# The seventh image pair's rows scattered as pieces as well, and two gathers and sums begun some steps sooner

## The reference

```
h = tok(x)                                    # patch embedding, bias, positions
h = h + attn(layernorm(h))                    # 8 heads, softmax of K over tokens, of Q over channels
z = layernorm(h); logits = z @ gate_w + gate_b
top 2 of 16 experts per token, weights renormed to 1
out = h + sum over the two of  weight * ((silu(z @ w1[e]) * (z @ w2[e])) @ w3[e])
```

## Time and profile before

| | us |
|---|---|
| three runs | 754.32, 754.61, 757.6 |
| median | 754.61 |
| the profiled execution's own time | 757.5 |
| its span, first to last instruction | 755.7 |
| POOL busy | 503.5 (67%) |
| PE busy | 622.1 (82%) |
| DVE busy | 476.6 (63%) |
| ACT busy | 353.2 (47%) |

### The profile page before, as it was taken

One profiled execution on the slowest core, in us unless ns is written; L12 is line 12 of the kernel. 1 busy time (PEld: TensorE's weight loads), 2 busy tenths in 40 slices (PEclk: granted clock), 3 DMA queues, 4 the chain that ended last, 5 costly groups with the idle time before them and its releaser, 6 DMA issues.

```text
span 755.7 us, 13960 instructions
## 1 busy us (share of the span) xinstructions
PE 622.1 (82%) x4059; PEld 519.8 (69%) x4059; DVE 476.6 (63%) x1322; ACT 353.2 (47%) x774; POOL 503.5 (67%) x537
## 2 busy tenths in 40 slices
PE   5886687788979998999889998998894888799328
PEld 3365454666568967886779687967884787798228
DVE  5654645567556677767666756766585687598410
ACT  2121311226355647564656456545562557486400
POOL 4362044757577477777777777777777777777773
PEclk9958778589989999999999989998998789898755
DMA  3499504134184329542844284537351635664322
GB/s 82 90 175 345 203 29 111 49 108 120 56 226 132 95 55 230 136 131 65 208 134 131 62 204 120 135 82 165 92 149 57 164 98 158 175 150 98 68 59 59
DMA packets 169200, 94.52 MB, mean 125 GB/s; under 512 B 99551, under 2 KB 153207, under 8 KB 169129
## 3 DMA queue, kind: packets, MB, share of 16 engines
q1 hardware_dynamic: 152728, 67.65, 34.5%
q0 software_dynamic: 15616, 25.59, 12.8%
q10 hardware_dynamic: 784, 0.39, 0.2%
HBM read 45.40 MB, written 48.18 MB: 124 GB/s over the span
## 4 chain that ended last, share of the span: by engine, by line
PE 51%; DVE 20%; issue 9%; POOL 7%; DMA 6%; ACT 5%; ACTq 0%; SPq 0%; POOLq 0%; DVEq 0%
PE h_ps L1593 8%; PE wide_ps L1381 7%; PE y_ps L1614 5%; PE hidT_ps L1606 4%; PE turn_ps L1571 3%; PE wide_ps L1401 3%; DMA hx<-xi_scratch 2%; PE wide_ps L1504 2%; DVE twice_y L1298 2%; POOL rows_scratch L674 2%; POOL kexp L691 2%; POOL hx L691 2%; DMA xi_scratch<-xi 2%; PE wide_ps L1387 2%; ACT sums L860 2%
## 5 line engine op out<-in xcount | busy, mean ns | idle before, releaser
L674 POOL DMA_INDIRECT rows_scratch<-z_parts,place x224 | 224.5, 1002 | 126.9 <-issue 64.9
L691 POOL DMA_INDIRECT sums<-y_scratch,place x192 | 185.1, 964 | 66.2 <-issue 56.4
L1593 PE MATMUL h_ps<-w_hi,rowsT 128*128 (+1 forms) x388 | 117.8, 330 | 15.8 <-DVE hid_all L1300 15.4
L1298 DVE SCALAR_TENSOR_TENSOR twice_y<-tanh,h_ps 128x256 f32<-128x256 f32 (+1 forms) x194 | 80.4, 414 | 52.5 <-ACT tanh L818 31.2
L1593 PE MATMUL h_ps<-w_lo,rowsT 128*128 (+1 forms) x388 | 105.6, 298 | 0.0
L1614 PE MATMUL y_ps<-w_sb,hidT_all 128*128 (+1 forms) x776 | 103.1, 279 | 1.4 <-ACT twice_y L833 1.4
L1614 PEld LDWEIGHTS y_ps<-w_sb,hidT_all 128*128 128x128 f32 (+1 forms) x776 | 100.2, 202 | 2.3 <-issue 2.3
L1593 PEld LDWEIGHTS h_ps<-w_hi,rowsT 128*128 128x128 f32 (+1 forms) x388 | 78.8, 203 | 25.9 <-issue 22.3
L818 ACT ACTIVATE tanh<-h_ps 128x256 f32<-128x256 f32 (+1 forms) x194 | 69.6, 386 | 46.5 <-PE h_ps L1593 42.6
L1300 DVE SCALAR_TENSOR_TENSOR hid_all<-twice_y,h_ps 128x256 f32<-128x256 f32 (+1 forms) x194 | 81.6, 421 | 6.7
L1571 PE MATMUL turn_ps<-ident,rows_all 128*128 128x128 f32 (+1 forms) x388 | 64.4, 292 | 21.0 <-DMA rows_all<-rows_scratch 14.2
(11 more groups left out here) (350 smaller groups left out, 1107.0 us busy)
## 6 DMA issues: line engine op xcount, KB each, us to landing
rows_all<-rows_scratch SPq DMA_DIRECT2D x84, 256.0 KB
y_scratch<-twice_y SPq DMA_DIRECT2D x84, 128.0 KB
rows_scratch<-tanh SPq DMA_DIRECT2D x3, 3276.0 KB
xi_scratch<-xi SPq DMA_DIRECT2D x16, 256.0 KB
hx<-xi_scratch SPq DMA_DIRECT2D x14, 256.0 KB
rows_scratch<-z_parts,place POOLq DMA_INDIRECT x224
out<-sums SPq DMA_DIRECT2D x56, 64.0 KB
x_in<-in_x SPq DMA_DIRECT2D x26, 128.0 KB
```

Source lines behind the costliest of these rows:

```text
L674: gp.indirect_dma_start(rows_dram[n], bass.IndirectOffsetOnAxis(ap=place[m % RING][:, r, j:j + 1], axis=0), z_parts[m % 2][:, j // 2, j % ...
L691: gp.indirect_dma_start(y_of[r][apart(m)][:, j // 2, j % 2, :], None, y_dram[m % 3][0:GROUPS[m] * GROUP * width(m), :], bass.IndirectOffse ...
L1298: ve.scalar_tensor_tensor(twice[0:w, j, :], tanh[0:w, j, :], 1.0, halves[:, j, 0, :], ALU.add, ALU.mult).then_inc(S["twice_done"], 1)
L1593: mm = te.matmul(h_ps[0:w, j * 256:(j + 1) * 256], rowsT[g % 2][:, j * w:(j + 1) * w], w12[:, bass.ds(experts[g][j], 1), :, :].rearrange(" ...
```

## The change

The seventh pair (m = 6) joins PIECED. Its 32 row scatters become 16 piece scatters, one every half step from half step 169 (steps 85 to 92), where pair 7 keeps two every half step from 196. It gets 13 groups instead of 12, so START[7] is 85, there are 98 groups and the loop is a step longer. It is still gathered and summed in the old way, from tiles of 126 rows.

Pair 7's embedding and attention fill `wide_ps` in steps 79 to 91, so pair 6's piece columns are formed in `turn_ps` (even columns, right after `project_in`) and `hidT_ps` (odd columns, at the step's end). `turn` and `turn_hidden` now wait until ACT has copied the piece out, and `take_piece` stands ahead of `copy_hidT` on ACT. The start of each piece (`find_moves` on DVE) is taken out of `find_pieces` and, for pair 6, worked out half a step ahead of it, in `hidT_ps`; pair 6's sort ends two steps later than before (ends 19.5 for 17.5, owner 20 for 18), pair 7's mean is 1.5 steps later.

GATHER: pair 4's begins in step 86 instead of 91, pair 5's in 98 instead of 102, pair 6's stays at 111, pair 7's moves to 124. SUMS: pair 4's quarters are in steps 94 to 97 (99 to 102 before), pair 5's in 107 to 110 (112 to 115 before), pair 6's and 7's a step later. GATES is a step later.

```diff
-PIECED = (7,)
+PIECED = (6, 7)
...
-         LATER, LATER, LATER, LATER, LATER._replace(tiles=17.5, bases2=18, ends=18.5, owner=19))
+         LATER, LATER, LATER, LATER._replace(tiles=17.5, bases2=18.75, moves=19, ends=19.5, owner=20),
+         LATER._replace(mean=8, means=8.5, tiles=17.5, bases2=18, moves=18.5, ends=18.5, owner=19))
...
-ROUTES = (None, None, None, None, None, None, None, 196)
-
-GATES = 105
+ROUTES = {6: (169, 1), 7: (196, 2)}
+
+GATES = 106
...
-SCATTER = (16, 22, 28, 44, 59, 72, 85, None)
-GATHER = (38, 51, 65, 78, 91, 102, 111, 123)
-SUMS = ([[43 + 14 * m + q for q in range(4)] for m in range(5)]
-        + [[112, 113, 114, 115], [121, 122, 122, 123], [124, 125, 126, 127]])
+SCATTER = (16, 22, 28, 44, 59, 72, None, None)
+GATHER = (38, 51, 65, 78, 86, 98, 111, 124)
+SUMS = ([[43 + 14 * m + q for q in range(4)] for m in range(4)]
+        + [[94, 95, 96, 97], [107, 108, 109, 110], [122, 123, 123, 124], [125, 126, 127, 128]])
...
-        def piece_place(j):
-
-            return wide_ps[:, j % 2 * 512:(j % 2 + 1) * 512]
+        def in_between(m):
+
+            return m < PAIRS - 1
+
+        def piece_place(m, j):
+
+            return (turn_ps, hidT_ps)[j % 2][:, :] if in_between(m) else wide_ps[:, j % 2 * 512:(j % 2 + 1) * 512]
...
-                wait(pe, "route_ready", j + 1)
-                wait(pe, "piece_ready", j - 1)
+                if in_between(m):
+
+                    wait(pe, *(("rowsT_ready", g + 2), ("hidT_ready", g))[j % 2])
+                wait(pe, "route_ready", i + 1)
+                wait(pe, "piece_ready", i - 1)
...
                 wait(pe, "rowsT_ready", g)
+                wait_pieces(2 * (g - 2 + LAG) - 1)
...
                 wait(pe, "hidT_ready", g)
+                wait_pieces(2 * (g + LAG))
+                if g + LAG == step_of(PIECED[0], 18):
+                    wait(pe, "moves_ready", 2)
...
                 if 0 <= g < GROUPS_ALL:
                     activate(g)
+                for m, j in routes_at(2 * s - 1):
+                    take_piece(m, j)
                 if 0 <= g - 1 < GROUPS_ALL:
                     copy_hidT(g - 1)
```

More of the change, by code:

```diff
@@ L288, in vit_kernel @@
         moves = placed[0]
-        piece_at = sb("piece_at", [P, COLS], U32)
+        piece_at = [sb(f"piece_at{n}", [P, COLS], U32) for n in range(2)]
         piece_from = sb("piece_from", [P, COLS], U32)
@@ L309, in vit_kernel @@
         flat = (w_patch[:, :, :, :].rearrange("p j t e -> p (j t e)"), x_in0[:, :, :].rearrange("p r f -> p (r f)"),
-                x_cols0[:, :, :].rearrange("p j c -> p (j c)"), squares[:, :])
-        pieces = [place[:, n * one:(n + 1) * one] for place, count in zip(flat, (10, 2, 2, 2)) for n in range(count)]
-        assert len(pieces) == COLS and one == PIECE * P
+                x_cols0[:, :, :].rearrange("p j c -> p (j c)"))
+        pieces = [[place[:, n * one:(n + 1) * one] for place, count in zip(flat + (last,), (10, 2, 2, 2)) for n in range(count)]
+                  for last in (base0[:, :, :, :].rearrange("p t b e -> p (t b e)"), squares[:, :])]
+        assert len(pieces[0]) == COLS and one == PIECE * P
         x_in = (x_in0[:, :, :], twice_y[:, :].rearrange("p (r f) -> p r f", r=2))
@@ L359, in vit_kernel @@
         scattered = [sem(f"scattered{n}") for n in range(3)]
-        pieces_out = sem("pieces_out")
+        pieces_out = [sem(f"pieces_out{n}") for n in range(len(PIECED))]
         rows_in = [sem(f"rows_in{n}") for n in range(3)]
@@ L388, in routes_at @@
                 for j in range(COLS):
-                    if ROUTES[m] + j // 2 == half:
+                    if ROUTES[m][0] + j // ROUTES[m][1] == half:
                         yield m, j
@@ L835, in take_piece @@
             def take_piece(m, j):
-                wait(act, "piece_ps_ready", j + 1)
-                if j == 0:
+                wait(act, "piece_ps_ready", COLS * nth(m) + j + 1)
+                if j == 0 and nth(m) == 0:
                     wait(act, "emb_ps_ready", 2 * PAIRS)
+                    wait(act, "x_turned", PAIRS)
+                elif j == 0:
+                    wait_scattered(act, PIECED[0])
+                    wait(act, "logits_ps_ready", PAIRS)
+                if j == COLS - 4:
                     wait(act, "mean_ps_ready", PAIRS)
-                    wait(act, "x_turned", PAIRS)
-                    wait(act, "logits_ps_ready", PAIRS)
-                sc.activation(pieces[j][0:PIECES, :], piece_place(j)[0:PIECES, 0:PIECE * 2 * E], ACT.Copy).then_inc(S["piece_ready"], 1)
+                if j == COLS - 2:
+                    wait(act, "h2_ready", 3 * PAIRS)
+                sc.activation(pieces[nth(m)][j][0:PIECES, :], piece_place(m, j)[0:PIECES, 0:PIECE * 2 * E], ACT.Copy).then_inc(S["piece_ready"], 1)
             def take_gates(j):
@@ L847, in take_gates @@
                     wait_scattered(act, PAIRS - 1)
-                sc.activation(pieces[j][0:PIECES, :], piece_place(j)[0:PIECES, 0:PIECE * P], ACT.Copy).then_inc(S["gates_turned"], 1)
+                sc.activation(pieces[1][j][0:PIECES, :], piece_place(PAIRS - 1, j)[0:PIECES, 0:PIECE * P], ACT.Copy).then_inc(S["gates_turned"], 1)
             def weigh(m, q):
@@ L1200, in find_past, with find_moves @@
                 ve.tensor_scalar(past[:, :], tile_id[:, :], ends[:, 0:1], None, ALU.is_ge).then_inc(S["past_ready"], 1)
+            def find_moves(m):
+                i = nth(m)
+                wait(dve, "base_ps_ready", m + 1)
+                wait(dve, "place_summed", 2 * m)
+                wait(dve, "moved_ready", i)
+                lbs = piece_place(m, 1)[0:PIECES, :].rearrange("p (n j e) -> p n j e", n=2, e=EXPERTS)
+                ve.tensor_scalar(moves[0:PIECES], lbs[:, 0], piece_id[0:PIECES, 0:1], None, ALU.is_le).then_inc(S["moves_ready"], 1)
+                wait(dve, "moves_ready", 2 * i + 1)
+                ve.tensor_tensor(moves[0:PIECES], moves[0:PIECES], lbs[:, 1], ALU.mult).then_inc(S["moves_ready"], 1)
+                wait(dve, "moves_ready", 2 * i + 2)
+                wait(dve, "piece_at_ready", i)
+                ve.tensor_reduce(moved[0:PIECES, :], moves[0:PIECES], AX_X, ALU.add).then_inc(S["moved_ready"], 1)
             def find_places(m):
@@ L1230, in find_pieces @@
                 i, side_ps = nth(m), sides[second(m)]
+                wait(dve, "slot_u_ready", i)
                 wait(dve, "place_ready", m)
@@ L1624, in _ @@
                     project_in(g)
+                for m, j in routes_at(2 * s - 1):
+                    move_rows(m, j, g)
                 if 0 <= g - 1 < GROUPS_ALL:
```

83 lines of the change are left out of this document (43 added, 40 removed).

## The result

The changed kernel takes 778.2 us (771.04 to 786.32) where the kernel before, run beside it, takes 754.54: ratio 1.0272, 95% interval 1.017 to 1.0374. The ratio leaves out the run of 786.32, which lies more than 1.5% above the fastest; the other three have the median 774.03. It is slower; whether by 2% or more, the interval leaves open. The profiled execution is the one of 782.37 us, span 780.6, the longest of these three. In the traces of this document POOL's first pair-6 issue lies anywhere from 532.77 to 541.95 us, with the same tables ahead of it, so times counted from the start of the span differ by some 9 us from trace to trace, and lengths counted from that issue are the safer comparison.

The account below looks back on a forecast made before the run. POOL's full queue was taken to bound the kernel, with PE tied to it at two turns. Pair 7's turn at 678.7, then 17.6 + 4.9 + 40.3 + 30.18, gave span 771.7; less 2.9, plus 1.8: 771 us, range 757 to 782.

Parts of the forecast that it names:

- the rival of the worst banks: Steps 85 to 92 each grow by the full 2.6 us and pair 4's sums show fully: 781, chance 0.17.
- the two terms for the sums: Moved sums delay pair 7's first piece by 0 to 6.5 us (3.2 taken) and pair 6's gather by 4.9 (high 6.5).
- POOL is full, and its queue's order feeds PE: POOL's queue decides the end, PE waits for it at two turns; 22.1 us less POOL work turns into idle stretches.
- Pair 6's last piece: Steps 85 to 92: issued at 594.4 at the earliest, behind 15 pieces and 28 gathers, plus 2.6 us lateness (0 to 8).
- the third rival: Exchanging the two banks costs the worst: 781, chance 0.17; its sign is steps 85 to 92 taking over 62 us together.
- From the last piece to the turn: From pair 6's last piece to PE's turn of step 93: 5.66 us; turn at 602.7, bounds 599.4 and 608.
- From the turn to pair 7's first piece: From step 93's turn: 25.6 us as before plus 3.2 for pair 4's sums; piece at 631.5 (625.0 to 640.1).
- Pair 7's pieces among pair 5's gathers: 15 pieces and 18 gathers ahead of pair 7's last piece: 41.55 us, before 19.06; PE loses 31 us at the turn.
- The end: Pair 6's gather 17.6 plus 4.9 us after pair 7's turn, its 32 gathers 40.3, then 30.18: span 771.7.
- DVE against POOL: The 32 added DVE operations slow POOL's pair 6 pieces by 4 us at most; the skill's rule implied 8.
- A full POOL: Rival: POOL stays full, so the whole 22.1 us come off; span 733.6, time 732.5, chance 0.05.
- No change: Rival: the loss fits PE's slack, pair 7's first piece 18 us after step 93's turn; time 756, chance 0.08.

Follow-up runs that it names:

- the new order: Changed kernel with gathers of pairs 4 and 5 by columns, spread among and behind the pieces: 760.98 us; with the even piece later in its step, 749.91.
- the order back: Changed kernel with gathers and sums of the fifth and sixth pairs in the earlier kernel's steps: 771.83 us; with the even piece later too, 757.26.
- the best order found: Changed kernel with gathers of pairs 4 and 5 spread by columns and the even piece later in its step: 749.91 us, ratio 0.9948.

## Why the prediction was right, and where its size was off

The direction, the chain and the range (757 to 782) held. The forecast of 771 was 7 us short of the median of all four runs (778.2) and 3 us short of that of the three in the ratio (774.03), so the times don't tell it from the rival of the worst banks (781). The trace does, step by step; it is of an execution of 782.37 us, so its errors are the larger ones. That the time stayed in the range is in part luck: step 93's turn, at 615.0, lies 7 us past the prediction's upper bound of 608, and what saved the range is that the two terms for the sums, 6.5 us each at the high end, came out at 1.6 and 2.4. By the steps of the prediction:

- **POOL is full, and its queue's order feeds PE.** Right. POOL lost its 22.1 us of work. Of the idle stretches two were forecast with a size, 28 and 9 us, and came at 26.96 and 5.79; the third, at the pieces, was put into the lateness of 2.6 us and came at 12.5.
- **Pair 6's last piece: mis-sized, and this is the term that failed.** Forecast 594.4 + 2.6 = 597.0, with a lateness of 0 to 8; measured 609.26. POOL came to step 85 one us later than before and idled 12.5 us on pieces. The forecast took POOL's need for a pair of steps, 15 to 18 us, to say that PE is mostly ahead. That counts the gathers as cover; but ahead of the first gather in POOL's program stand four pieces with nothing between them, and there POOL needs 5 us for what took PE two steps (533.13 to 553.74). The growth of the eight steps was too small as well: 21 us was its worst case, 26.7 came. The worst case of 2.6 us a step is DVE's and ACT's added work. It leaves out PE's own added 1.0 us a step, though the same sentence works it out (the 48 matmuls of L1570 took 8.1 us), and PE's waits early in its step for ACT's copy of the rows, which the diff names (the wait on `rowsT_ready`), and for DVE's matrices, 12.8 us together, and PE's lower clock. The prediction's own sign for the third rival, over 62 us for these steps, was met with 69.8: as to the banks that rival was nearer than the forecast, and short as well. The experiments show which part is which: the place of the piece in its step is worth 13 of the 26.7 us. Of the whole time it is worth 11 us with the new order (760.98 to 749.91) and 15 with the order back (771.83 to 757.26); with the order as changed the difference (778.2 to 769.57) is not clear of the spread.
- **From the last piece to the turn**, 5.66 forecast, 5.74 measured: 2.55 for the scatter to land, 3.13 for the load.
- **From the turn to pair 7's first piece**, 28.8 forecast, 615.00 to 642.19 = 27.2 measured. If all of the 1.6 us over the 25.6 before are pair 4's sums, they show by that, not by 3.2, and not by the 6.5 that the third rival took.
- **Pair 7's pieces among pair 5's gathers**, 41.55 forecast, 683.88 - 642.19 = 41.69 measured; turn 5.63 later. The step with the most weight in the loss of PE's slack was exact.
- **The end.** Pair 6's gather at the turn + 20.0 (22.5 forecast), its 32 issues to 750.35 in 40.9 (40.3), the rest 30.25 (30.18). The errors add up: 12.3 - 1.6 + 0.1 - 2.5 + 0.6 + 0.1 = 9.0, which is 780.6 less 771.7, within rounding.
- **DVE against POOL.** Pair 6's pieces now run beside 32 added DVE operations. The piece scatters' durations (ns, min/median/max), before and now (ten pieces of pair 7; ten each of pairs 6 and 7):

```profile
L661 POOL DMA_INDIRECT rows_scratch<-w_patch,piece_at x10: 904/920/1166, 623.1 to 634.9; - x10
L667 POOL DMA_INDIRECT rows_scratch<-w_patch,piece_at x20: 907/930/1559, 541.3 to 664.0; - x20
```

The medians agree; one of the twenty took 1.56. The rule of the Trainium skill that was weighed there (SBUF — State Buffer, Who interferes with whom), that such a DVE operation and a GpSimd one shut each other out for the whole instruction, would have made it up to 8 us. The added operations of 0.52 us don't show it: away from longer DVE operations, POOL's issues beside them took 0.91 to 1.06. Operations of 1.22 us that are in both kernels do. From 300 us to pair 7's gather, 11 of POOL's issues in either trace took over 1.3 us, and each ran beside a TENSOR_TENSOR of 1024 columns with two SBUF inputs (11 of 13 such operations in either), as here on POOL and DVE of the changed kernel:

```profile
594.37 1.88 POOL L697 DMA_INDIRECT sums<-y_scratch,place  x1 [0.30 <-issue]
594.21 1.23 DVE L1111 TENSOR_TENSOR z_parts<-z,z_parts 128x1024 fp32r<-128x1024 f32 x1 [5.19 <-ACT z_parts L803]
```

POOL's issues beside a TENSOR_REDUCE of 1024 columns, which has one input, took 0.94 to 0.98. So the long operations with two inputs go with a DMA issue held back by 0.4 to 1.0 us; why the short ones don't, no run shows. The change adds none of the long ones, and the 4 us at most that the prediction allowed for DVE did not come.
- **The rivals.** A full POOL (732.5) needs its idle time to be nil; the best order found still leaves 17.3 us. No change (756) needs pair 7's first piece 18 us behind step 93's turn; it came 27 behind.

## What to carry to other kernels

An engine whose track looks 67% busy can be full: look at the gaps between its instructions before counting what an edit frees. Where such an engine issues in program order both what another engine waits for and what nobody needs yet, count what stands ahead of the awaited transfer, in units of one issue; that count gave the turns within 1 us where the order alone was changed, and missed by some 5 us in two of the kernels in which POOL waited for single pieces. A thin spread of the unurgent issues took the loss of 2.7% to 0.7%, and together with the later piece to a gain of 0.5%. Two delays that the same transfer waits for don't add up: undoing one shows little until the other is gone. Before a bank that is exchanged between two uses is put first in a step, look who must empty it and what that engine does first; moved behind the step's independent work, the same exchange cost 12 to 13 us less in eight steps.

## What was not expected of the hardware

The same 363 matmuls of steps 85 to 92 took 53.16 us of PE's time in the changed kernel and 46.98 with the piece later in the step, while the granted clock of the stretch was 0.86 and 0.94 of full speed. By the ratio of the clocks alone 4.4 of these 6.2 us would come (an estimate from these numbers). With the early piece PE stood idle ahead of single matmuls up to 3.3 us at a time (the longest wait for L813), with the later one up to 2.1. So up to half of the 13 us that the early place cost is slower work at a lower clock, not waiting. It came back in all four kernels with the early piece and pair 6's pieces (0.86 in each, 69.3 to 69.8 us) and was gone in the four with the later one (0.94 to 0.97, 54.9 to 57.4 us).

Which wait brings the lower clock is not shown. Cut into stretches of 4.2 us, the changed kernel's trace has the clock at full speed (2.4 GHz) from 549.93 to 583.53, at 0.95 to 587.73, where PE was busy for 1.54 us of the 4.2, and at 0.50 (1.2 GHz) to 591.93, then at 0.50 to 0.74 to the end of step 92. But it was at full speed through the stretch from 554.13 to 558.33 and the next, though PE was busy for only 0.92 us of the first.
